# Second scan of a fused state-space and mixture block: residual sums taken tile by tile, convolution products and the state projection at other pairs

## The reference

```python
proj = hidden @ W_in.T;  x, gate = proj[..., :1024], proj[..., 1024:]
xc = conv_b + sum(conv_w[:, j] * xpad[:, j:j + L, :] for j in range(4))
x = silu(xc)
ssm = x @ W_x.T                      # 32 + 16 + 16 columns, each part rms-normed
dt = softplus(ts @ W_dt.T + b_dt)
state = state * exp(dt_t * A) + (dt_t * u_t) * B_t     # over 512 steps, 16 states
y = (state * C_t).sum(n) + x * D;  y = y * silu(gate);  out = y @ W_out.T
```

## Time and profile before

| | |
|---|---|
| median of 3 runs | 855.61 us (855.35 to 856.38) |
| the profiled execution | 856.99 us, of which the span is 855.2 us |
| DVE busy in the span | 692.5 us (81%) |
| PE busy | 697.4 us (82%) |
| POOL busy | 495.4 us (58%) |
| ACT busy | 459.2 us (54%) |
| first and last start of the scan instruction | 66.0 and 490.1 us |

### The profile page before, as it was taken

The page is one execution under the profiler, slowest core; times in us unless marked ns, Lnnn a source line. Parts: engine busy times, 40 slices in busy tenths (PEclk is TensorE's granted clock), DMA queues, the critical chain, the costliest instruction groups (busy, mean ns, idle before and its releaser), DMA issues. The chain is left out here.

```text
span 855.2 us, 8287 instructions
## 1 busy us (share of the span) xinstructions
PE 697.4 (82%) x2732; PEld 321.5 (38%) x2732; DVE 692.5 (81%) x699; ACT 459.2 (54%) x772; POOL 495.4 (58%) x259
## 2 busy tenths in 40 slices
PE   5989679998696878357539588987999978999894
PEld 4533123332122222011113133433445435787773
DVE  5779899999999999979999989993464655486658
ACT  3556687787547675775554445672343344422331
POOL 1419999989999999999999800300001122330152
PEclk9999779999878989567659889999999989999998
DMA  9223312333426443423325059740130020000011
GB/s 287 46 94 135 123 58 71 119 123 110 168 70 209 136 146 124 136 98 123 103 78 188 0 157 251 208 139 1 24 124 1 18 81 2 1 0 1 1 50 49
DMA packets 40946, 82.40 MB, mean 96 GB/s; under 512 B 6711, under 2 KB 8160, under 8 KB 40648
## 3 DMA queue, kind: packets, MB, share of 16 engines
q1 hardware_dynamic: 40904, 81.87, 30.4%
HBM read 70.65 MB, written 11.21 MB: 96 GB/s over the span
## 5 line engine op out<-in xcount | busy, mean ns | idle before, releaser
L2135 POOL TENSOR_TENSOR dbu<-rep_du,bc 128x1024 f32<-128x1024 f32 x128 | 299.4, 2363 | 2.3 <-ACT rep_du L1832 1.4
L1703 ACT ACTIVATE psum<-rep_dt,aneg 128x512 f32<-128x512 f32 x256 | 166.1, 682 | 125.5 <-DVE hc L1109 105.2
L1098 DVE TENSOR_TENSOR_SCAN psum<-psum,dbu 128x1024 f32<-128x1024 f32 x87 | 198.8, 2285 | 10.2 <-ACT psum L1703 9.6
L881 PE MATMUL psum<-hc,stk 128*32 128x512 f32 x512 | 87.5, 762 | 58.7 <-POOL hc L2144 30.4
L1109 DVE TENSOR_TENSOR hc<-psum,bc 128x1024 f32<-128x1024 f32 x87 | 106.5, 1224 | 3.4 <-PE psum L881 0.4
L2144 POOL TENSOR_TENSOR hc<-hc,bc 128x1024 f32<-128x1024 f32 x41 | 96.6, 2357 | 8.8 <-DVE hc L1098 8.6
L1098 DVE TENSOR_TENSOR_SCAN hc<-psum,dbu 128x1024 f32<-128x1024 f32 x41 | 93.5, 2281 | 4.7 <-PE psum L881 2.8
L658 PE MATMUL psum<-xf_hi,gu_hi 128*128 128x512 f16 x176 | 68.3, 388 | 1.5 <-ACT sg L1977 1.0
L658 PE MATMUL psum<-xf_lo,gu_hi 128*128 128x512 f16 x176 | 68.0, 387 | 0.0
L658 PE MATMUL psum<-xf_hi,gu_lo 128*128 128x512 f16 x176 | 68.0, 386 | 0.0
L2213 POOL TENSOR_TENSOR h<-h 128x512 f32<-128x512 f32 x16 | 18.9, 1178 | 72.9 <-ACT h L2063 72.9
(11 more groups left out here) (256 smaller groups left out, 1451.5 us busy)
## 6 DMA issues: line engine op xcount, KB each, us to landing
rep_dt<-rep_scratch SPq DMA_DIRECT2D x60, 256.0 KB, 3.4
rep_du<-rep_scratch SPq DMA_DIRECT2D x60, 256.0 KB, 4.4
cw<-c_scratch SPq DMA_DIRECT2D x11, 768.0 KB, 8.5
qw<-qgu_in SPq DMA_DIRECT2D x11, 512.0 KB, 5.3
bc<-bc_scratch SPq DMA_DIRECT2D x16, 256.0 KB, 4.5
rep_scratch<-du_t SPq DMA_DIRECT2D x15, 256.0 KB, 2.0
rep_scratch<-dt_t SPq DMA_DIRECT2D x15, 256.0 KB, 2.3
qw<-qd_in SPq DMA_DIRECT2D x11, 256.0 KB, 6.9
```

The lines of the kernel that those rows point to most:

```text
L881: last = pe.matmul(y_rows(k), stk[:], hc[:, (i + k // 2) % HCS, k % 2, :], start=False, stop=(s == GN - 1))
L1098: dve.tensor_tensor_scan(h, a, dbu[:, i % DBS].rearrange("p e t -> p (e t)"), 0.0, ALU.mult, ALU.add)\
L1703: last = act.activation(psum[:, 2 * (i % 2) + e, :], rep_dt[:, cc % 2, k, :], ACT.Exp, scale=aneg[:, k, c, n:n + 1])
L2135: pool.tensor_tensor(dbu[:, i % DBS], rep_du[:, cc % 2, k:k + 2, :], bc[:, n, :].unsqueeze(1).broadcast_to([P, 2, L]), ALU.mult).then_inc( ...
```

## The change

The items x, cv, ssm and gate of batch 1 stand at other steps, and the residual's sums and squares are spread: one tile per pair at pairs 91 to 94 and 95 to 98, root at 99, where before there were two tiles per pair at pairs 90 to 93 and the root at 94. No instruction is added or removed; nothing changes on VectorE or POOL.

```diff
-        (2, 1): [("x", 1, 1), ("cv", 1, 0)], (2, 2): [("cv", 1, 1)], (2, 3): [("x", 1, 2)],
-        (3, 0): [("x", 1, 3), ("cv", 1, 2)], (3, 1): [("x", 1, 4), ("cv", 1, 3)], (3, 2): [("cv", 1, 4)],
-        (3, 3): [("x", 1, 5)], (4, 0): [("x", 1, 6), ("cv", 1, 5)], (4, 1): [("x", 1, 7), ("cv", 1, 6)],
-        (4, 2): [("cv", 1, 7)], (5, 0): [("gate", 1, 0)], (5, 1): [("ssm", 1)], (5, 2): [("gate", 1, 1)],
-        (5, 3): [("ms", 1)],
+        (2, 1): [("x", 1, 1)], (2, 2): [("cv", 1, 0), ("x", 1, 2)], (2, 3): [("cv", 1, 1)],
+        (3, 0): [("x", 1, 3), ("cv", 1, 2)], (3, 1): [("x", 1, 4)], (3, 2): [("cv", 1, 3)],
+        (3, 3): [("x", 1, 5), ("cv", 1, 4)], (4, 0): [("x", 1, 6), ("cv", 1, 5)], (4, 1): [("x", 1, 7)],
+        (4, 2): [("cv", 1, 6)], (4, 3): [("cv", 1, 7)], (5, 0): [("gate", 1, 0)], (5, 1): [("gate", 1, 1)],
+        (5, 2): [("ssm", 1)], (5, 3): [("ms", 1)],
...
-                if i in (last + 12, last + 13):
-                    sums(2 * (i - last - 12))
-                    sums(2 * (i - last - 12) + 1)
-                if i == last + 14:
-                    less_mean()
-                    squares(("ffn", 0), 0, x[:, 0, :])
-                    squares(("ffn", 0), 1, x[:, 1, :])
-                if i == last + 15:
-                    squares(("ffn", 0), 2, x[:, 2, :])
-                    squares(("ffn", 0), 3, x[:, 3, :])
+                if last + 13 <= i < last + 13 + NT:
+                    sums(i - last - 13)
+                if last + 17 <= i < last + 17 + NT:
+                    t = i - last - 17
+                    if t == 0:
+                        less_mean()
+                    squares(("ffn", 0), t, x[:, t, :])
...
-                if i == last + 16:
+                if i == last + 21:
                     own_root(("ffn", 0), fnmr, fnmr_ready)
```

## The result

The changed kernel takes 863.21 us (median of 6 runs, 862.35 to 864.82); the kernel before took 856.85 us beside it (6 runs, 855.35 to 858.53). By the medians that is 6.4 us slower, where 4.4 were forecast. The ratio, estimated from all the runs and not as the quotient of the two medians, is 1.0079, 95% interval 1.0065 to 1.0093. The profiled execution took 864.23 us, its span 862.4, 7.2 more than the span of before.

The account below looks back on a forecast made before the run. VectorE was taken to set the pace in the pair loop. Terms 0.2 + 1.5 + 1.3 + 1.1 + 1.7 + 1.0 - 2.4 = 4.4 us slower, so 855.61 + 4.4 = 860.0 us; range 852.5 to 863.5.

Parts of the forecast that it names:

- TensorE's clock behind x 6 and ssm: After TensorE's idle times ahead of x 6 and ssm its clock falls: 1.7 us and 1.0 us lost.
- Pairs 20 to 31: Pair loop, batch 1's first convolutions: old wait at pair 22 goes, new ones at 24 and 30; 0.2 us lost.
- about 1.0 us: Wait at pair 30 for decay(30), passed on from x 3's lateness, where 0.6 us stood in all.
- Pairs 32 to 38: Pair loop: x 6's bank wait behind silu_u(0) makes 5.4 us of holes at pairs 34 and 36; net 1.5 us lost.
- The first rival: Pairs 32 to 38: silu hidden, so the bank wait and its clock loss go; 852.9 us, chance 0.17.
- the clock that holds: Rival: TensorE's clock doesn't fall behind x 6 and ssm; 1.7 us slower, 857.3 us, chance 0.15.
- Pairs 43 to 49: Pair loop: silu_u(1) delays decay(44), 1.3 us lost; ssm's later bank delays normed_ssm(1), 1.1 us lost.
- the forecast chain of 7.6 us: ScalarE's work from pair 41's product through silu_u(1) to decay(44), against VectorE's 6.2 us.
- ssm at half clock throughout: Rival: all 16 ssm matmuls run at half clock; 5.4 us above the forecast, 865.4 us, chance 0.07.
- The residual: Pairs 91 to 94: 4.8 us of ScalarE waits go, a 2.3 us POOL wait comes; 2.4 us gained.
- POOL doesn't bind at pair 93: Rival at the residual: no POOL wait, so all 4.8 us are gained; 857.6 us, chance 0.08.
- The rule weighed against the trace: silu table switches: some 1380 ns of drain each, by estimate 2.8 us more for two, making 862.8 us.

Follow-up runs that it names:

- e10: e7 with block 0's convolution moved to step (2, 2), ahead of block 1's; 852.85 us, 0.9949 of the kernel before.
- e3: The changed kernel with two neighbouring items swapped, block 5's convolution ahead of x 6; 859.81 us, 1.0037 of the kernel before.
- e4: The changed kernel with silu_u(0) one pair later, at pair 34, behind take_conv(4); 859.02 us, 1.0032 of the kernel before.
- e6: The changed kernel with POOL adding only 16 of 512 columns of residual tiles 2 and 3; 862.77 us, 1.0067 of the kernel before.
- e2: The kernel before with only the items x, cv, ssm and gate moved, residual as before; 867.04 us, 1.0119 of the kernel before.
- e7: The kernel before with the residual part, silu_u(0) one pair later and cv 6 moved to step (4, 2); 852.76 us, 0.9953 of the kernel before.
- e5: The changed kernel with ssm back at step (5, 1) and gate 1 at (5, 2); 860.60 us, 1.0040 of the kernel before.
- e11: e1 run again unchanged: the kernel before with only the residual part; 856.88 us, 0.9991 of the kernel before.
- e1: The kernel before with only the residual's sums, squares and root changed, moved items as before; 856.94 us, 1.0001 of the kernel before.
- e12: e1 once more unchanged, for a third profile; one run, 854.91 us.
- e9: The changed kernel with the edits of e3, e4 and e5 together; 856.66 us, 0.9994 of the kernel before.
- e8: The kernel before, run again unchanged for a second profile; 856.53 us, 0.9992 of the kernel before.

## Where the prediction was right, and where its sum failed

863.21 us lies within the range I gave, by 0.3 us, but against the 856.85 measured beside it the loss is 6.4 and not 4.4. The forecast was slower, and slower it is, and every wait that was named came, at its pair and on its engine. What failed is the sum. It undersized the convolution part and the chain of pairs 43 to 49, and it priced TensorE's clock behind x 6 and ssm alone and put everything else at nothing, where the clock cost another 0.5 us in the loop and 0.6 behind it. Its terms, one by one, from the table of differences:

- **Pairs 20 to 31: mis-sized**, 0.2 forecast (its own figures, 0.6 + 1.0 - 0.9 - 0.6, give 0.1), 0.7 measured. "About 0.6 us at pair 24" came (0.59), and so did x 3's wait of "about 0.7" (0.74 in TensorE's timeline). But from there "about 1.0 us" at pair 30 was 1.49: x 3 started 1.08 us later than before, and ScalarE's decay(30) behind it 1.2 us later, while the scans that it had to meet stood 0.15 us earlier. I had counted the new wait, not the lateness that x 3 already had when it came to it. e10 shows the same trade without the wait for the bank.
- **Pairs 32 to 38 with x 6's clock: right**, 1.5 + 1.7 = 3.2 forecast, 3.3 measured. The holes were 2.64 (forecast 2.5) and 4.45 (2.9 + 1.7). e3 and e4 took them away from either end, e3 with x 6 back at 3.70 us. The first rival, a covered bank wait, is thereby excluded, and so is the clock that holds. (That rival's limit, a chain of 14.2 us, was set too high: VectorE's own work is 13.2 us.)
- **Pairs 43 to 49: mis-sized**, 1.3 + 1.1 + 1.0 = 3.4 forecast, 4.2 measured. The wait of 1.48 at pair 44, 1.6 in VectorE's row, is the forecast chain of 7.6 us (decay(43) starts at 212.28, decay(44) ends at 219.88) and two hand-overs between the engines of 0.1 us each, which it left out. In pair 48 1.14 + 1.46 = 2.6 came, 2.7 in the row, instead of 2.1: ssm's 8.99 us were 0.2 more than "7.1 + 1.7", and some hand-overs of 0.04 to 0.14 us add 0.3. "The gate and everything else of this step lies beside VectorE" was wrong for the state sum behind ssm: pair 48's product waited for it. But that wait is a part of the 2.6 and adds nothing to it, since the root that `normed_ssm` needs came later still, at 239.24. ssm at half clock throughout (14.2 us) did not occur.
- **The residual: right in the loop**, 2.4 forecast, 2.4 measured in the changed kernel, with POOL's 2.36 us for the 2.3 forecast; e6 shows that it hangs on the length of POOL's adds. "POOL doesn't bind at pair 93" is excluded.
- **Put at nothing:** 0.5 us between pairs 72 and 91, which e2, e6 and e7 show too and e3, e4 and e5 don't, and 0.7 us behind the loop. The first is the clock again. After 2.07 us of idle time the granted clock was 0.58 over the next 2 us and 0.79 over 4 more, the output projection took 8.15 us (TensorE's timeline below) where it takes 7.13 before, in e3 and in e5, and pair 81's small product waited 0.41 us for the state sum behind it. In e5 TensorE had stood for 2.53 us there and the clock held. The second is the clock too, for 0.6 of 0.7 us, by the two stretches under e11.

```profile
337.51 8.15 PE L658 MATMUL psum<-wout,g 128*128 128x512 f32 x16
```

0.5 + 0.1 + 0.8 + 0.5 + 0.7 = 2.6 more, and the profiled span is 7.2 us longer where 4.4 were forecast (the rest is rounding and the 0.1 us by which the loop started later). By medians it is 6.4.

The rule weighed against the trace, the Trainium skill's ScalarE: Activation LUTs, "What ACT_TABLE_LOAD costs", with some 1380 ns of drain for a switch, would, as an estimate, have come to 862.8 us and so nearer to the measurement. That would have been luck: the row after the table load stands at 177.26, 0.02 us behind the load's end at 175.96 + 1.28, and neither load starts more than 0.02 us behind the work ahead of it. The trace disagrees with it here, and the loss is found in the terms above.

**What stays open.** The residual part makes the loop 2.2 to 2.8 us shorter in three profiles, and yet e1 and e11 as a whole run in the time of before (1.0001 and 0.9991). The profiles of e11 and e12 show where the gain was given back, and that the granted clock behind the loop was lower in both. That this happens in most runs of this kernel is what the spread of e1's runs suggests (two near 854.7, nine from 856.15 up); the mean clock over each whole run, 0.906 and 0.902 for the two and 0.898 to 0.904 for the nine, doesn't tell them apart clearly; why its clock should fall there more often than that of the kernel before, no run here tells. With e7, where 4.2 us go from the loop, 4.4 arrive in the time.

## What to carry to other kernels

When work moves later in one in-order queue, follow two things in every other: who now stands ahead of the next user of the same bank, and how late the mover already was. Of 13.2 us of waits here the largest, 4.45, came from a bank that ScalarE freed behind a 4.5 us silu, and swapping two neighbours in TensorE's list took it away. A stall on TensorE can bring a slower clock for what follows it, 1.7 us for x 6, and the clock can fall far from the moved items too, as it did ahead of pair 81. A wait removed can come back in part as a wait for the next engine in line: at pair 93 POOL, without a pause in its row there, took back 2.4 of 4.8 us. A high busy share alone doesn't say so: in pairs 24 to 45, with POOL busy for 49.5 of 50 us before, e9 has no wait on it. A gain of 2 us inside the loop is no gain in the time until it is timed, since the clock of the stages behind it varies by as much from profile to profile.

## What the runs showed of the hardware

- TensorE's granted clock after idle time: 0.52 after 3.67 us (8 matmuls in 5.39 instead of 3.70 us), 0.50 and then 0.83 after 6.85 us (16 in 8.99; in 9.48 in e3 and e4 after the same time). After 2.55 us, with the same 14 us of work ahead, 16 took 7.08 us in e5 (clock 1.00) and 8.78 in e9 (0.63 over the first 4 us). The price of a fall was 1.6 to 2.4 us (1.6 from the earlier trace rows and e5's 7.08: 0.9 on the state sum and 0.7 on ssm), and the longest idle time had both 8.99 and 9.48.
- The same matmuls at the same distance behind the loop had granted clocks of 0.50 to 0.73, and 89 us further on 0.69 to 0.88, in 14 profiles. Within one kernel (e1 and e11) the clock in these two stretches makes 2.3 of the 2.8 us by which the part behind the loop differs (364.6 to 367.4 us).
- The loop of before repeated in e8 to 0.06 us at every pair; that of e1 took 421.9, 421.6 and 421.2 us in three profiles. Most steps at single pairs repeat to a tenth between kernels; those at pairs 8 to 24, which differ by up to 0.6 us, and those that hang on TensorE's clock (pair 36 by 0.2, pair 49 by 0.5, pair 82 by 0.5) don't. Differences of the whole time could be read to no better than 2 us from one profile each.
